# Key-value sums of a linear attention: a Gram matrix of tokens and features, multiplied by the value weights once, in place of value products per token tile

## The reference

```python
k = _heads(hidden_states @ k_w.T + k_b, b, s)
v = _heads(hidden_states @ v_w.T + v_b, b, s)
kp = jax.nn.elu(k) + 1.0
kv = jnp.einsum('bhsd,bhse->bhde', kp, v)
z = jnp.einsum('bhsd,bhd->bhs', qp, kp.sum(axis=2))[..., None]
attn = jnp.einsum('bhsd,bhde->bhse', qp, kv) / (z + EPS)
```

## Time and profile before

| | us |
|---|---|
| median of 3 runs | 1527.58 (1522.91 to 1531.15) |
| the profiled execution | 1524.45 |
| its span | 1522.7 |
| PE busy in the span | 1459.6 (96%) |
| DVE busy | 1032.7 (68%) |
| ACT busy | 755.7 (50%) |
| POOL busy | 464.3 (30%) |
| first matmul of `stage_keys` | 8.0 |
| first matmul of `stage_experts` | 146.87 |

### The profile page before, as it was taken

How to read it: one execution, slowest core, us unless ns; L and a number is a source line. 1 busy time by engine, 2 the same in 40 slices (tenths; PEclk the granted TensorE clock), 3 DMA queues, 4 the chain that set the end, 5 groups by cost and what they waited for, 6 DMA issues and landing times. The chain is left out here.

```text
span 1522.7 us, 23559 instructions
## 1 busy us (share of the span) xinstructions
PE 1459.6 (96%) x6981; PEld 1057.1 (69%) x6981; DVE 1032.7 (68%) x2942; ACT 755.7 (50%) x1283; POOL 464.3 (30%) x697
## 2 busy tenths in 40 slices
PE   6999999999999999999989999999999997998998
PEld 4778788888777888788855555555555555787776
DVE  6453666666658646887867986665668985668592
ACT  5633555655565544433335555555555553234561
POOL 0000577777620112323221222221212214053062
PEclk9999999999999999999979999999999999999999
DMA  5001222222100434376698505315145028743021
GB/s 188 1 1 46 106 92 76 79 110 76 56 28 28 135 108 121 118 202 194 189 238 307 120 6 123 77 53 122 31 97 122 5 81 255 220 168 140 30 82 14
DMA packets 107076, 161.53 MB, mean 106 GB/s; under 512 B 12656, under 2 KB 63744, under 8 KB 100704
## 3 DMA queue, kind: packets, MB, share of 16 engines
q1 hardware_dynamic: 103548, 153.58, 33.5%
q0 software_dynamic: 1024, 2.43, 0.8%
q10 hardware_dynamic: 2404, 4.33, 0.8%
HBM read 117.44 MB, written 42.87 MB: 105 GB/s over the span
## 5 line engine op out<-in xcount | busy, mean ns | idle before, releaser
L2253 ACT ACTIVATE l_pt<-banks 128x1024 f32<-128x1024 f32 (+3 forms) x288 | 218.4, 810 | 140.1 <-PE banks L2124 138.0
L2328 DVE CUSTOM_DVE_ANT_0 stage<-banks,l_edges 128x384 f32<-128x384 f32 (+2 forms) x374 | 197.6, 544 | 79.6 <-issue 78.6
L2164 PE MATMUL banks<-l_pt,l_v 128*64 128x512 f32 (+3 forms) x1152 | 222.0, 507 | 0.4 <-POOL l_pt L2227 0.3
L718 POOL TENSOR_TENSOR ex_hl<-ex_h,ex_hh 128x512 fp32r<-128x512 f32 x128 | 165.3, 1297 | 81.4 <-ACT ex_hh L686 81.3
L2226 POOL TENSOR_TENSOR l_turn<-l_before 128x2 f32<-128x2 f32 x192 | 38.5, 200 | 379.2 <-ACT l_pt L2253 352.5
L751 DVE SCALAR_TENSOR_TENSOR ex_rw<-banks,ex_wb 128x512 f32<-128x512 f32 x128 | 88.3, 691 | 79.0 <-PE banks L75 78.9
L2331 DVE TENSOR_REDUCE l_mx<-banks 128x1 f32<-128x384 f32 (+1 forms) x204 | 111.3, 546 | 33.1 <-PE banks L2102 32.5
L686 ACT ACTIVATE ex_hh<-ex_h 128x512 fp32r<-128x512 f32 x128 | 80.9, 632 | 103.6 <-DVE ex_h L759 102.5
L2164 PEld LDWEIGHTS banks<-l_pt,l_v 128*64 128x64 f32 x1152 | 69.5, 138 | 89.6 <-issue 69.7
L73 PE MATMUL banks<-ex_xlh,ex_wh 128*128 128x512 f32 x256 | 101.6, 397 | 2.0 <-DVE ex_rw L751 2.0
L74 PE MATMUL banks<-ex_xll,ex_wh 128*128 128x512 f32 x256 | 99.8, 390 | 0.0
(11 more groups left out here) (473 smaller groups left out, 3508.2 us busy)
## 6 DMA issues: line engine op xcount, KB each, us to landing
ex_wb<-gates_by_expert SPq DMA_DIRECT2D x16, 1024.0 KB, 4.7
layer_qk<-qkv_yh SPq DMA_DIRECT2D x32, 256.0 KB, 3.2
layer_qk<-qkv_yl SPq DMA_DIRECT2D x32, 256.0 KB, 3.6
layer_v<-qkv_vs SPq DMA_DIRECT2D x15, 512.0 KB, 4.6
l_v<-layer_v SPq DMA_DIRECT2D x7, 1024.0 KB, 17.7
ex_ws<-ew_in SPq DMA_DIRECT2D x16, 384.0 KB, 5.1
l_q<-layer_qk SPq DMA_DIRECT2D x12, 512.0 KB, 7.8
l_k<-layer_qk SPq DMA_DIRECT2D x12, 512.0 KB, 13.8
```

The source lines that it names most:

```text
L718: pool.tensor_tensor(hl[:, k % RING, :], h[:, k % RING, :], raw(hh[:, k % RING, :]), ALU.subtract).then_inc(hl_done, 1)
L2164: last = pe.matmul(bank[h * 2 * HD:(h + 1) * 2 * HD, (qa - b * BT) * P:(qz + 1 - b * BT) * P], v[par][:, kt, h, :], pt[:, step_part(b, j), ...
L2253: act.activation(pt[:, step_part(b, j), :, 0:width], G.banks[:, 2 * slot:2 * slot + 2, 0:width], ACT.Exp, scale=scale).then_inc(p_done, 1)
L2328: dve.tensor_tensor_reduce(cutoff[:, n % 4, 0:width], G.ps[5 + n % MB][:, 0:width], masked, 1.0, NEG, ALU.add, ALU.max, mx[:, h, m, c:c + ...
```

## The change

The value product per tile goes, and with it the sums of line 319. In its place PE adds the outer product of the normalised tile and its features to a Gram matrix, `kp` against `n`: for each group of 128 of the 512 features of `n` an `mm3` of 128x512, 12 matmuls per tile, into four banks (2, 4, 5 and 1), which are held from tile 0 to tile 15. It does so two tiles late (`gram(t - 2)`). For this the normalised tile is needed with the tokens on the partitions in high and low parts: POOL, which now has a program, makes both (`token_split`). The features are split too: ACT the high part (`feature_high`), DVE the low part (`feature_low`). POOL adds up the features (`feature_total`). After tile 15 the Gram matrix is split (ACT and DVE, four pieces each) and `products` makes the sums: four FP32 matmuls of the features' total with the value bias and ones, then 48 fp32r matmuls of 128x128.

With four banks held, keys have one bank, bank 0, but for tile 1: key product `t` waits until the bias add of tile `t - 1` has read it. Tiles are normalised in place, so the ring `xn` goes with its wait. The value weights are loaded last, and split at tiles 7 and 9.

```diff
-    K, V, SMALL, SUMS, XT = (0, 1), 2, 3, (4, 5), (6, 7)
+    GRAM, SMALL, SUMS, XT = (2, 4, 5, 1), 3, (6, 7), (6, 7)
...
+        def key_bank(t):
+            return pss[GRAM[NC - 1]] if t == 1 else pss[0]
...
             load_tokens(sp, G, I, 2)
             sp.dma_start(kbb[:, :], I["k_b"].partition_broadcast(P)).then_inc(bias_in, 16)
-            sp.dma_start(vbb[:, :], I["v_b"].partition_broadcast(P)).then_inc(bias_in, 16)
             load_tokens(sp, G, I, 3)
             load_tokens(sp, G, I, 4)
+            sp.dma_start(gb[:, :], I["biases"].partition_broadcast(P)).then_inc(gb_in, 16)
+            sp.dma_start(vbb[:, :, 0:P], I["v_b"].partition_broadcast(P).rearrange("p (g n) -> p g n", g=NC)).then_inc(vb_in, 16)
             weights.load(sp, 4, None)
-            sp.dma_start(gb[:, :], I["biases"].partition_broadcast(P)).then_inc(gb_in, 16)
...
             def keys(t):
                 if t >= 2:
-                    pe.wait_ge(kx_ready, t - 1)
+                    pe.wait_ge(kx_ready, 1 if t == 2 else t)
...
-            def values(t):
-                if t >= 1:
-                    pe.wait_ge(v_ready, t)
-                mm3(pe, pss[V], [(x(t, c), w("v", c)) for c in range(NC)]).then_inc(v_mm, 1)
+            def gram(t):
+
+                if t == 0:
+                    pe.wait_ge(kx_ready, 2)
+                pe.wait_ge(xl_ready, t + 1)
+                pe.wait_ge(kl_ready, t + 1)
+                for c in range(NC):
+                    cols = slice(c * P, (c + 1) * P)
+                    last = mm3(pe, pss[GRAM[c]], [((xh[:, t % 2, cols], xl[:, t % 2, cols]), (kh[:, t % 2, :], kl[:, t % 2, :]))],
+                               start=t == 0, stop=t == NT - 1)
+                last.then_inc(gram_done, 1)
...
-            def sums_of(t):
-
-                pe.wait_ge(kp_ready, t + 1)
-                pe.wait_ge(v_ready, t + 1)
+            def products():
+
+                pe.wait_ge(total_ready, NT)
+                pe.wait_ge(vb_in, 16)
+                pe.wait_ge(ones_made, 1)
                 for g in range(NC):
-                    last = pe.matmul(sum_of(g), kp[:, t % 2, g * P:(g + 1) * P], vv[:, t % 2, g, :],
-                                     start=t == 0 and g in (0, NC - 1), stop=t == NT - 1, skip_group_check=True)
+                    pe.matmul(sum_of(g), total[:, g * P:(g + 1) * P], vbb[:, g, :], start=g in (0, NC - 1), stop=False,
+                              skip_group_check=True)
+                weights.ready(pe, 3)
+                for c in range(NC):
+                    pe.wait_ge(gl_ready, c + 1)
+                    wh, wl = w("v", c)
+                    for g in range(NC):
+                        cols = slice(g * P, (g + 1) * P)
+                        last = mm3(pe, sum_of(g)[:, 0:P], [((gh[:, c, cols], gl[:, c, cols]), (wh[:, cols], wl[:, cols]))],
+                                   start=False, stop=c == NC - 1, skip_group_check=True)
                 last.then_inc(kv_done, 1)
...
             keys(1)
-            weights.ready(pe, 1)
             for t in range(NT):
                 if t >= 2:
                     keys(t)
                 if 2 <= t < AHEAD:
                     transposes(2 * t + 2)
                     transposes(2 * t + 3)
-                values(t)
-                if t >= 1:
-                    sums_of(t - 1)
+                if t >= 2:
+                    gram(t - 2)
...
-            sums_of(NT - 1)
+            gram(NT - 2)
+            gram(NT - 1)
+            products()
...
+            def feature_high(t):
+                act.wait_ge(kp_ready, t + 1)
+                if t >= 2:
+                    act.wait_ge(gram_done, t - 1)
+                act.activation(kh[:, t % 2, :], kp[:, t % 2, :], ACT.Copy).then_inc(kh_ready, 1)
...
                     high(2 * t + 3)
+                if t >= 1:
+                    feature_high(t - 1)
                 if t + 1 < AHEAD:
                     normal(2 * t + 4)
-                if t in (0, 2):
-                    weights.high(act, 4 + t // 2, 5 + t // 2)
+                if t in (AHEAD, AHEAD + 2):
+                    n = 4 + (t - AHEAD) // 2
+                    weights.high(act, n, n + 1)
...
+            act.wait_ge(gram_done, NT)
+            for c in range(NC):
+                act.activation(gh[:, c, :], pss[GRAM[c]], ACT.Copy).then_inc(gh_ready, 1)
+
+        @block.gpsimd
+        def _(pool):
+            pool.memset(vbb[:, :, P:W1], 1.0).then_inc(ones_made, 1)
+
+            def token_split(t):
+                pool.wait_ge(xn_ready, t + 1)
+                if t >= 2:
+                    pool.wait_ge(gram_done, t - 1)
+                pool.tensor_copy(xh[:, t % 2, :], X[:, t, :]).then_inc(xh_ready, 1)
+                pool.wait_ge(xh_ready, t + 1)
+                pool.tensor_tensor(xl[:, t % 2, :], X[:, t, :], raw(xh[:, t % 2, :]), ALU.subtract).then_inc(xl_ready, 1)
+
+            def feature_total(t):
+                pool.wait_ge(kp_ready, t + 1)
+                if t == 0:
+                    pool.tensor_copy(total[:, :], kp[:, 0, :]).then_inc(total_ready, 1)
+                else:
+                    pool.wait_ge(total_ready, t)
+                    pool.tensor_tensor(total[:, :], total[:, :], kp[:, t % 2, :], ALU.add).then_inc(total_ready, 1)
+
+            pool.wait_ge(ones_made, 1)
+            token_split(0)
+            token_split(1)
+            for t in range(NT):
+                feature_total(t)
+                if t + 2 < NT:
+                    token_split(t + 2)
...
-                dve.tensor_tensor(kx[:, t % 2, :], pss[K[t % 2]], kbb[:, :], ALU.add).then_inc(kx_ready, 1)
+                dve.tensor_tensor(kx[:, t % 2, :], key_bank(t), kbb[:, :], ALU.add).then_inc(kx_ready, 1)
+                if t >= 1:
+                    feature_low(t - 1)
                 if t < AHEAD:
                     low(2 * t + 2)
                     low(2 * t + 3)
-                dve.wait_ge(v_mm, t + 1)
-                if t >= 2:
-                    dve.wait_ge(kv_done, t - 1)
-                dve.tensor_tensor(vv[:, t % 2, :, 0:P], pss[V].rearrange("p (c n) -> p c n", c=NC),
-                                  vbb[:, :].rearrange("p (c n) -> p c n", c=NC), ALU.add).then_inc(v_ready, 1)
                 dve.wait_ge(e_ready, t + 1)
                 dve.wait_ge(r_ready, t + 1)
+                if t >= 2:
+                    dve.wait_ge(total_ready, t - 1)
                 dve.tensor_tensor(kp[:, t % 2, :], ke[:, t % 2, :], kr[:, t % 2, :], ALU.add).then_inc(kp_ready, 1)
...
+            feature_low(NT - 1)
+            for c in range(NC):
+                dve.wait_ge(gh_ready, c + 1)
+                dve.tensor_tensor(gl[:, c, :], pss[GRAM[c]], raw(gh[:, c, :]), ALU.subtract).then_inc(gl_ready, 1)
```

More of the change, by code:

```diff
@@ L213, in stage_keys @@
     logit_ready, p1 = G.sem("kv_logit"), G.sem("kv_exp")
-    k_mm, v_mm, kx_ready, e_ready, r_ready = (G.sem("kv_" + n) for n in ("k_mm", "v_mm", "kx", "e", "r"))
-    kp_ready, v_ready, kv_done, link = (G.sem("kv_" + n) for n in ("kp", "v", "done", "link"))
+    k_mm, kx_ready, e_ready, r_ready = (G.sem("kv_" + n) for n in ("k_mm", "kx", "e", "r"))
+    kp_ready, kv_done, link = (G.sem("kv_" + n) for n in ("kp", "done", "link"))
+    kh_ready, kl_ready, xh_ready, xl_ready, total_ready, gram_done, gh_ready, gl_ready, ones_made, vb_in = (
+        G.sem("kv_" + n) for n in ("kh", "kl", "xh", "xl", "total", "gram", "gh", "gl", "ones", "vb_in"))
     bias_in, gate_done, wt_mm, wt_sb = (G.sem("kv_" + n) for n in ("bias", "gate", "wtmm", "wtsb"))
@@ L229, in stage_keys @@
         ve, sd, rstd, shift = (M.sb(n, [P, NT]) for n in ("ve", "sd", "rstd", "shift"))
-        xn = M.sb("xn", [P, RING, D])
-        kbb, vbb, gb = M.sb("kbb", [P, D]), M.sb("vbb", [P, D]), M.sb("gb", [P, EXPERTS])
+        kbb, gb = M.sb("kbb", [P, D]), M.sb("gb", [P, EXPERTS])
         kx, ke, kr = M.sb("kx", [P, 2, D]), M.sb("ke", [P, 2, D]), M.sb("kr", [P, 2, D])
-        kp, vv = M.sb("kp", [P, 2, D]), M.sb("vv", [P, 2, NC, W1])
+        kp, vbb = M.sb("kp", [P, 2, D]), M.sb("vbb", [P, NC, W1])
+        kh, kl = M.sb("kh", [P, 2, D], F32R), M.sb("kl", [P, 2, D], F32R)
+        xh, xl = M.sb("xh", [P, 2, D], F32R), M.sb("xl", [P, 2, D], F32R)
+        total = M.sb("total", [P, D])
+        gh, gl = (nc.alloc_sbuf_tensor_at("kv_g" + n, [P, NC, D], F32R, offset=G.X_at + at * D * 4)
+                  for n, at in (("h", NT // 2), ("l", NT // 2 + NC)))
         gz, gp = M.sb("gz", [P, NT, EXPERTS]), M.sb("gp", [P, NT, EXPERTS])
@@ L295, in keys @@
                         pe.wait_ge(weights.w_lo, c // 2 + 1)
-                        last = mm3(pe, pss[K[0]], [(x(0, c), w("k", c))], start=c == 0, stop=c == NC - 1)
+                        last = mm3(pe, key_bank(0), [(x(0, c), w("k", c))], start=c == 0, stop=c == NC - 1)
                     last.then_inc(k_mm, 1)
                 else:
-                    mm3(pe, pss[K[t % 2]], [(x(t, c), w("k", c)) for c in range(NC)]).then_inc(k_mm, 1)
```

(26 more changed lines are left out.)

14 lines of the change are left out of this document (7 added, 7 removed).

## The result

The changed kernel takes 1533.47 us (median of 14 runs, 1530.22 to 1535.76), the kernel before 1525.45 us in 14 runs of the same series (1521.74 to 1531.15). The ratio is 1.0053, with a 95% interval of 1.0044 to 1.0062. 1534 us were forecast beside a kernel before of 1527.58; the profiled execution took 1530.92 us, with 1531.0 forecast. As a difference, 6.5 us were forecast; the medians differ by 8.0 (6.7 to 9.5 by the interval), the two profiled executions by 6.5.

A forecast was written before the change was run, and what follows sets the result against it. PE was taken to bound the first stage; what the sums save is spent by key product 12, and moved Grams and tail products add up to +6.5 us: 1531.0 profiled, 1534 beside 1527.58. Range 1527 to 1541.

The forecast's parts named there:

- What bounds the kernel, and what leaves: First stage: PE sets the pace; 13.3 us of sums go, value and Gram products cost the same 2.72 us.
- The start: Before key product 3: normalisations 1.7 us earlier, a DVE and POOL collision +1.0; key product 3 at 44.1 against 45.27.
- POOL and DVE: Tile loop: POOL takes 3.2 of 5.44 us; a DVE two-input op and POOL op collide, one waits, 0 to 1.3 us.
- The gates: Between key products 9 and 10: PE idles 6.2 us for DVE's bias add, 2.1 from collisions; low clock 1.65 more.
- The roots' wait: Before key product 12: PE waits 1.4 us for the bias add behind DVE's roots, and 0.5 for collisions.
- The end: After key product 12: last Gram ends at 145.9, 48 products take 5.3 us, next stage at 153.5 against 146.9.
- Sum: Whole kernel: +6.5 us, 1531.0 on the profiled execution's own time, 1534 beside 1527.58.
- my own line of 7.6: Whole kernel: 0.5% (7.6 us) can be told from no change; chances slower 0.37, same 0.58, faster 0.05.
- (a): After the last Gram: 128-column products cost what 512-column ones do, 10.9 in place of 5.3; +12.1 us, chance 0.12.
- (b): Tile loop: POOL becomes the pace, 0.7 us over 14 tiles; +16 us, 1544, chance 0.06.
- (c): Start, gates and roots: no lock, and no low clock at the gates; +1.2 us, 1529, chance 0.20.
- (d): Start: half of some 8 us of PE wait filled, products at 0.07: +0.6 us, with (c) -4.7; chance 0.12.

The follow-up runs named there:

- experiment 9: Kernel before with three of the four sums left out in 14 of 16 tiles: 1519.30 us, ratio 0.9967.
- experiment 7: Changed kernel, POOL's first split held until DVE has split the first key weights: 1529.97 us; second kernel, instead another order of PE's start: 1531.51 us.
- experiment 2: Changed kernel with POOL's split of tile 9 and all behind it held until DVE is through with the gates: 1531.18 us, ratio 1.0034.
- experiment 3: Changed kernel with 21 products that nothing reads, run by PE while it waits for the gates: 1531.99 us, ratio 1.0047.
- experiment 4: Changed kernel with two key banks by turns from tile 9: 1533.06 us; second kernel, also tile 8's features' low part before the gates: 1532.46 us.
- experiment 6: Changed kernel with ACT's copy of the turned gates ahead of its three feature ops: 1531.41 us in a single run.
- experiment 1: Kernel before with only the single key bank of the change, values and sums as they were: 1528.07 us, ratio 1.0022.

## Why the prediction was right, point by point

**What bounds the kernel, and what leaves.** Right. PE sets the pace in the first stage; experiment 9 takes sums off PE and the stage shrinks by what they cost there, less new waits. The sums were priced somewhat low: from key product 3 to 9 the change saves 51.32 - 46.07 = 5.3 us with 4.9 forecast. POOL's and ACT's added work is hidden: POOL waits 61 us in total for Grams between 40 and 146 us, and PE never for POOL.

**The start.** The mechanism was right, the end 1.2 us too late: key product 3 at 42.87, not 44.1, and at 43.62 in the latest of the eight executions with this start. The collision came as forecast (2.21 us in place of 1.23), and experiment 7 shows it. The normalisation of tile 5 ended at 30.35 where the forecast, with the collision in it, was 31.1, and that of tile 7 at 39.57 where it was 40.6; from there to key product 3 passed 3.3 us with 3.5 forecast. So the mis-sized part is the chain ahead of the normalisations; which of its steps I took too long stays open. The waits (0.87, 2.74, 2.56, 1.12) add to 7.3 us where I had some 8.

**POOL and DVE.** "One waits out the other" is what happens. Over 16 tiles the mean of DVE's feature sum (two inputs in SBUF) rises to 902 ns and of its low part to 818, from 0.69 us without a neighbour; the bias add, with one input in PSUM, stays at 690:

```profile
L589 DVE TENSOR_TENSOR kv_kp<-kv_ke,kv_kr 128x512 f32<-128x512 f32 x16 | 14.4, 902 | 20.1 <-ACT kv_ke L410 13.3 <-ACT kv_kr L411 6.7
L526 DVE TENSOR_TENSOR kv_kl<-kv_kp,kv_kh 128x512 fp32r<-128x512 f32 x16 | 13.1, 818 | 8.2 <-ACT kv_kh L417 8.1
L579 DVE TENSOR_TENSOR kv_kx<-banks,kv_kbb 128x512 f32<-128x512 f32 x16 | 11.0, 690 | 17.9 <-PE banks L75 17.7
```

(Groups of DVE, 0 to 150 us: xcount | busy, mean ns | idle and its releasers.) The Trainium skill, under SBUF — State Buffer, "SBUF: two separate sides", counts a DVE op with two SBUF inputs among those that take the lock against a GpSimd op that reads SBUF. These three rows agree, and experiment 2 removes the collision by moving POOL's work alone.

**The gates.** Right in place, releaser and size: 5.84 us with 6.2 forecast, of which the lock 1.89 with 2.1 forecast. Mis-sized was the low clock: 2.2 us (experiment 3) where I took 1.65 from the earlier trace rows. The low clock there lasted for 3.4 to 3.7 us, here for nearly all of 5.0, and what it costs is half of what it lasts. The roots' wait was 0.93 with 1.9 forecast: at full clock key product 12 followed key product 10 after 12.2 us (experiment 3) with 12.8 forecast, and PE's four products between them took 11.3 in place of 10.9. What I had not seen is that the hole is DVE's and not the bank's (experiment 4). It changed no number of the forecast, but mending the bank alone would have been the wrong way: in the trace it gains 0.5 us.

**The end.** From key product 12 to the last Gram's end 31.2 us passed and I had 29.3. 1.3 of this is a wait that I did not foresee: ACT's copy of the turned gates stands behind three feature ops, one more copy has come ahead of those, and PE turns the next gates only when it is done (0.43 three times; experiment 6). The rest is 2.78 to 2.85 us per product in place of 2.72. Behind it, the path through ACT and DVE took 1.67 us (1.57 forecast), the 48 products 5.36 (5.3), the crossing to the next stage 0.32 (0.7).

**Sum.** 6.8 us to the next stage with 6.6 forecast, but errors of 1.2 to 1.9 us of both signs cancel in it, which is luck. Each single term is known to about 1 us, not to the 0.2 of the sum. That the profiled execution came within 0.1 us of its forecast is luck too: it lies 2.55 us below its kernel's median. By the medians the change costs 8.0 us, 1.5 more than forecast; the 1.2 us between that and the stage's 6.8 no profile here locates. As for the chances, 8.0 lies just beyond my own line of 7.6, on the side that I gave 0.37, but its interval begins at 6.7, so the runs do not decide between "same" and "slower" as I drew them.

**Rivals.** (a) dear products: excluded, 0.112 us each, where it decides from 0.135. (b) POOL as the pace: excluded, PE never waits for its split in the tile loop. (c) no lock and no low clock: excluded by experiments 2 and 3, which price the two at 1.9 and 2.2 us. (d) the start's idle time hidden: it was not; to hide a part of it took another order of PE's work (1.8 us of the 7.3 at key product 3).

## What to carry to other kernels

When the engine that paces a stage gets less to do per tile, look for the largest block of work that another engine does in one piece: what used to bridge it may be gone, and the gain goes into that gap, with the low clock on top. Cut such a block into pieces smaller than a tile's slack before adding buffers; a second bank only moved the stop to the next product that needs the same engine. Sums over tiles that end in a serial tail must win more than the tail: here 13.3 us of PE work left and 7.5 us stand behind the last tile where 1.4 stood.

## What the runs showed of the hardware beyond what I expected

The idle time alone did not tell whether the low clock comes, nor for how long. After 5.84, 3.95 and 3.81 us of waiting at the gates the next product was granted 0.53, 0.65 and 0.62. After 2.89 us in experiment 1 and 2.45 in the first kernel of experiment 4 it was 1.00. But the same 5.84 us in the second kernel of experiment 7 brought 0.65 (4.23 us for the key product in place of 5.03), and in the second kernel of experiment 4 the waits of 2.49 and 2.46 us brought 0.65 and 0.61 (4.41 us). The row of the 2.49 us case:

```profile
107.20:111.38 4.18, 4.18 (x12) 3.36 (x13) 2.38 (x3) 2.85 (x5) 0.00 (x0) 0.65 0.00 0
```

Ahead of the 2.49 us lay a wait of 0.66, 5.5 us earlier, but none lay so near ahead of the 2.46. Both come from the execution that was 7 us longer than its kernel's median. What tells the cases apart was not tested.

A 128x128 product with its own 128-column weights has a record of 0.28 us and is spaced 0.112, where the 512-column one is spaced 0.23: a quarter of the columns costs half the time. Its price stands with twice as many of them, so it is what this shape costs and no start-up.
